# Embedding look-ups in two passes over six small tables, and fourteen loads moved from SyncE's queue to ScalarE's

## The reference

```python
e = jnp.stack([tbl_0[ids[:, 0]], ..., tbl_38[ids[:, 38]]], axis=1)      # (2048, 39, 32)
conv1 = einsum('bid,bjd,ijk->bkd', e, e, W1)                            # 39*39 pairs -> 128
hidden1, final1 = conv1[:, :64], conv1[:, 64:]
conv2 = einsum('bid,bjd,ijk->bkd', e, hidden1, W2)                      # 39*64 pairs -> 128
z = sum(concatenate([final1, conv2], axis=1), axis=2)                   # (2048, 192)
h = relu(concatenate([z, dense_ctx], axis=1) @ W_top1 + b_top1)         # 512
h = relu(h @ W_top2 + b_top2)                                           # 256
y = h @ W_top3                                                          # 1
```

## Time and profile before

| | us |
|---|---|
| median of 3 runs | 811.2 (807.7 to 817.63) |
| the profiled execution | 808.5 |
| span of its core | 806.6 |
| PE busy | 739.2 (92%) |
| VectorE (DVE) busy | 697.9 (87%) |
| ScalarE (ACT) busy | 572.3 (71%) |
| GpSimd (POOL) busy | 543.3 (67%) |

### The profile page before, as it was taken

One profiled execution on the slowest core, in us unless ns is written; L12 is line 12 of the kernel. 1 busy time (PEld: TensorE's weight loads), 2 busy tenths in 40 slices (PEclk: granted clock), 3 DMA queues, 4 the chain that ended last, 5 costly groups with the idle time before them and its releaser, 6 DMA issues.

```text
span 806.6 us, 18279 instructions
## 1 busy us (share of the span) xinstructions
PE 739.2 (92%) x6938; PEld 431.1 (53%) x6938; DVE 697.9 (87%) x1142; ACT 572.3 (71%) x1535; POOL 543.3 (67%) x538
## 2 busy tenths in 40 slices
PE   2991787899999999999999999998999999999997
PEld 1660132375656565655556464655556565656576
DVE  6971986879999999899989898997999999999962
ACT  1330335768888888888887878786888888788883
POOL 6877777777777777777777777777777777700000
PEclk9995986899999999999999999999999999999999
DMA  6738878988898888989898889888898989888500
GB/s 194 233 66 221 241 189 235 254 244 250 253 235 248 239 257 232 262 237 247 228 255 244 243 240 242 241 235 243 232 252 237 252 234 265 248 252 249 158 2 2
DMA packets 135720, 179.32 MB, mean 222 GB/s; under 512 B 105304, under 2 KB 116518, under 8 KB 117648
## 3 DMA queue, kind: packets, MB, share of 16 engines
q1 hardware_dynamic: 111524, 166.84, 71.6%
q0 software_dynamic: 17088, 8.78, 6.6%
q10 hardware_dynamic: 7020, 2.52, 1.2%
HBM read 166.35 MB, written 16.71 MB: 227 GB/s over the span
## 4 chain that ended last, share of the span: by engine, by line
PE 29%; DVE 20%; DMA 20%; ACT 11%; SPq 8%; POOL 6%; issue 6%; ACTq 0%; DVEq 0%; POOLq 0%
DVE blocks L787 18%; DMA copies<-xt 16%; PE hidden L420 14%; SPq L350 7%; PE sums L473 6%; PE sums L447 6%; POOL emb L386 6%; ACT arena L636 5%; DMA xt<-emb 2%; DMA emb<-in_tbl,ids_tile 2%; ACT hid_high L605 2%; PE sums L478 2%; DVE turned L819 2%; ACT xdiag L624 2%; ACT hidden L613 1%
## 5 line engine op out<-in xcount | busy, mean ns | idle before, releaser
L386 POOL DMA_INDIRECT emb<-in_tbl,ids_tile x534 | 543.1, 1017 | 164.8 <-issue 112.5
L787 DVE TENSOR_TENSOR blocks<-copies 117x512 f32<-117x512 f32 x840 | 524.7, 693 | 75.5 <-DMA copies<-xt 59.7
L420 PE MATMUL hidden<-blocks,w_pairs 117*64 117x512 f32 x1792 | 434.6, 614 | 40.3 <-DVE blocks L787 38.4
L636 ACT ACTIVATE arena<-sums 64x480 f32<-64x480 f32 (+2 forms) x936 | 293.0, 313 | 138.6 <-PE sums L447 125.6
L420 PEld LDWEIGHTS hidden<-blocks,w_pairs 117*64 117x64 f32 x1792 | 152.1, 139 | 244.9 <-issue 105.5
L447 PEld LDWEIGHTS sums<-xdiag,turned 64*103 64x103 f32 x2000 | 101.5, 172 | 82.5 <-issue 46.1
L624 ACT ACTIVATE xdiag<-turned 32x468 f32<-32x468 f32 (+1 forms) x256 | 118.8, 464 | 25.7 <-DVE turned L763 22.6
L447 PE MATMUL sums<-xdiag,turned 64*103 64x78 f32 x2000 | 115.4, 262 | 3.3 <-ACT arena L636 2.2
L605 ACT ACTIVATE hid_high<-hidden 32x512 f32<-32x512 f32 x126 | 74.1, 588 | 11.6 <-PE hidden L420 9.7
L473 PE MATMUL sums<-arena,weights 128*64 128x128 f32 x1280 | 78.5, 279 | 0.0
L473 PEld LDWEIGHTS sums<-arena,weights 128*64 128x64 f32 x1280 | 71.1, 139 | 2.4
(11 more groups left out here) (50 smaller groups left out, 258.3 us busy)
## 6 DMA issues: line engine op xcount, KB each, us to landing
copies<-xt SPq DMA_DIRECT2D x448, 312.0 KB
emb<-in_tbl,ids_tile POOLq DMA_INDIRECT x534
xt<-emb SPq DMA_DIRECT2D x32, 152.0 KB
xt<-xt SPq DMA_DIRECT2D x16, 304.0 KB
xt<-emb SPq DMA_DIRECT2D x32, 104.0 KB
blocks<-hot_t SPq DMA_DIRECT2D x6, 512.0 KB, 6.1
xt<-emb SPq DMA_DIRECT2D x32, 56.0 KB
weights<-in_finals SPq DMA_DIRECT2D x1, 1728.0 KB
```

What stands on the lines that cost most here:

```text
L386: pool.indirect_dma_start(out=emb[u][:, f * D:(f + 1) * D], out_offset=None, in_=tables[f], in_offset=bass.IndirectOffsetOnAxis(ap=ids_til ...
L420: mm = nc.tensor.matmul(hidden[64 * c:64 * c + 64, k % 2, bank, :], w_pairs[0:ROWS, t, bank * HALF_HID:bank * HALF_HID + HID], blocks[0:RO ...
L636: op = nc.scalar.activation(out[:, :, cols].rearrange("p h (u b) -> p h u b", u=2), g[rows, i], ACT.Copy)
L787: op = nc.vector.tensor_tensor(blocks[0:ROWS, at + c, :], a[:, cols], b[:, cols], ALU.mult)
```

## The change

- Look-up j is now of table j % 6 and of the half j // 6: six look-ups serve the first 1,024 samples, then six the second. No columns are left out. All six tables are loaded at the start, each with its own place (`copies` 2, 3, 6 and 7), and split once.
- The first tile's hot columns come from the look-ups: ScalarE copies them into `emb[0]` (`hot_first`), and GpSimd gathers 33 tables for tile 0 too, without waits on look-ups.
- Index loads are one for each look-up, half as large, twelve in place of six, with eight buffers.
- There are two keeps, one for each half, in place of three; tile 1's hot rows need the first alone, tile 8's the second.
- The spill of tile 0 stands after all index loads. Within a spill the copy inside `xt` is issued ahead of the wait for the last part's gathers, in every tile.
- ScalarE issues the fourteen copies of chunk 1, after the keep of the second half, all look-ups and tile 0's spill; copy 4, with one buffer, comes last there and waits for step 0 of chunk 0. SP goes from chunk 0's copies to tile 1's hot rows and spill.
- One-hot place 1 is now `copies` 4 and 5; the places go round by three up to the last look-up, which takes place 0.

```diff
-ONES_PLACE = [j % 3 if j < COPIES_FREE else 2 if j % 2 == 0 else 0 for j in range(LOOKUPS)]
+TURNED_FREE = LOOKUPS - 3
+ONES_PLACE = [j % 3 if j < LOOKUPS - 1 else 0 for j in range(LOOKUPS)]
...
-                else:
-                    for m in range(2):
-                        sp.wait_ge(hot_kept[m], 16 * ((KEPT + 1 - m) // 2))
+                if tile in (1, TILES // 2):
+                    sp.wait_ge(hot_kept[tile // (TILES // 2)], 16)
...
-                    sp.wait_ge(gathered[u][s], 16 * gathers(tile, s))
+                    if s < len(PARTS) - 1:
+                        sp.wait_ge(gathered[u][s], 16 * gathers(tile, s))
                     if s == 0 and tile:
                         sp.wait_ge(hot_rows_loaded[u], 16 * hot_loads(tile))
+                    elif s == 0:
+                        sp.wait_ge(hot_first, N_HOT)
                     if s == len(PARTS) - 1:
                         sp.wait_ge(spilled_first[u], 16 * 2 * (p + 1))
...
+                        sp.wait_ge(gathered[u][s], 16 * gathers(tile, s))
...
-                elif chunk == 1:
-                    sp.wait_ge(hot_looked, COPIES_FREE)
-                elif v in (2, 3):
+                elif chunk == 1 or v in (2, 3):
                     sp.wait_ge(hot_looked, LOOKUPS)
...
                 load_hot_rows(1)
-                for v in LOAD_ORDER:
-                    load_copy(0, 0, 1, v)
                 spill(0, 1)
...
-            for f in range(F):
-                if f >= AT_ONCE:
-                    pool.wait_ge(hot_looked, (f - AT_ONCE) // A_LOOKUP + 1)
+            for f in range(N_HOT, F):
                 gather(0, f)
...
             def look_up(j):
-                n = j // 2
+                n = j % N_HOT
...
             def copy_rows(j):
-                n, h = j // 2, j % 2
+                n, h = j % N_HOT, j // N_HOT
                 act.wait_ge(hot_summed, j + 1)
-                if n >= 4 and n % 2 == 0 and h == 0:
-                    act.wait_ge(hot_kept[n // 2 % 2], 16 * (n // 4))
+                if h == 0:
+                    nc.scalar.activation(emb[0][:, n * D:(n + 1) * D], sums[:, j % 4, 0:D], ACT.Copy).then_inc(hot_first, 1)
...
+            def load_second_chunk():
+                act.wait_ge(spilled[0], 16 * SPILLS)
+                act.wait_ge(hot_looked, LOOKUPS)
+                for v in sorted(LOAD_ORDER, key=lambda v: len(x_copy[v]) == 1):
+                    if len(x_copy[v]) == 1:
+                        act.wait_ge(multiplied, pairs_done(0, COPY_USES[v][-1], BANKS - 1))
+                    for g, r in enumerate(ROTATION[v]):
+                        act.dma_start(x_copy[v][1 % len(x_copy[v])][g::THIRDS, :],
+                                      xt[0, r:r + F, 1, :]).then_inc(copied[v][1 % len(x_copy[v])], 16)
```

More of the change, by code:

```diff
@@ L138, in build @@
         y_col = sb("y_col", [P, TILES], F32)
-        rows = sb("rows", [P, 2, TILES, 2, D], F32)
+        rows = sb("rows", [P, 2, TILES // 2, N_HOT, D], F32)
         row_number = sb("row_number", [P, 18], F32)
@@ L176, in build @@
         hot_consts_loaded = sem("hot_consts_loaded")
-        hot_raw_loaded = [sem(f"hot_raw_loaded{n}") for n in range(2)]
+        hot_raw_loaded = [sem(f"hot_raw_loaded{n}") for n in range(N_HOT)]
         hot_unpacked = sem("hot_unpacked")
@@ L185, in build @@
         hot_copied = sem("hot_copied")
+        hot_first = sem("hot_first")
         hot_kept = [sem(f"hot_kept{m}") for m in range(2)]
@@ L258, in gathers @@
             part = PARTS[s]
-            each = part.stop - max(part.start, N_HOT)
-            return each * (tile // 2 + 1) if tile % 2 else part.stop - part.start + each * (tile // 2)
+            return (part.stop - max(part.start, N_HOT)) * (tile // 2 + 1)
         def hot_loads(tile):
@@ L278, in _, with index @@
             sp.wait_ge(hot_stored, 16)
[L280 to L283, removed]
+            def index(j):
+                if j >= INDICES:
+                    sp.wait_ge(ones_ready, ONES_BEFORE[j - INDICES + 1])
+                h = j // N_HOT
+                sp.dma_start(hot_index[j], hot_t[j % N_HOT, h * HALF_B:(h + 1) * HALF_B].partition_broadcast(P)
+                             ).then_inc(hot_index_loaded[j % INDICES], 16)
             def load_hot_rows(tile):
@@ L353, in first_tile @@
             def first_tile():
-                for n in range(N_HOT):
-                    index(n)
-                    if n == 1:
+                for j in range(LOOKUPS):
+                    index(j)
+                    if j == 3:
                         sp.dma_start(ids_tile[1][:, :], ids_t[1]).then_inc(ids_loaded[1], 16)
-                    if n == 4:
+                    if j == INDICES:
                         sp.dma_start(weights[:, 0:N_FIN], finals).then_inc(fin_loaded, 16)
-                    if n == 5:
+                    if j == INDICES + 1:
                         sp.dma_start(weights[:, N_FIN:], layers).then_inc(mlp_loaded, 16)
-                    spill(0, 0, [s for s in range(len(PARTS)) if FIRST_SPILLED[s] == n])
+                spill(0, 0)
                 sp.wait_ge(spilled[0], 16 * SPILLS)
@@ L391, in _ @@
             pool.wait_ge(ids_loaded[0], 16)
-            for f in range(F):
-                if f >= AT_ONCE:
-                    pool.wait_ge(hot_looked, (f - AT_ONCE) // A_LOOKUP + 1)
+            for f in range(N_HOT, F):
                 gather(0, f)
             pool.wait_ge(ids_loaded[1], 16)
-            for at, f in enumerate(range(N_HOT, F)):
-                pool.wait_ge(hot_looked, (F - AT_ONCE + at) // A_LOOKUP + 1)
+            for f in range(N_HOT, F):
                 gather(1, f)
@@ L533, in look_up @@
                     for bank in range(BANKS):
-                        skip = P if j % 2 == 0 and bank == 0 else 0
-                        mm = nc.tensor.matmul(hidden[0:3 * D, j % 2, bank, skip:512], upper[n][:, c, :],
-                                              hot_ones[j][:, c, bank * 512 + skip:(bank + 1) * 512],
+                        mm = nc.tensor.matmul(hidden[0:3 * D, j % 2, bank, :], upper[n][:, c, :],
+                                              hot_ones[j][:, c, bank * 512:(bank + 1) * 512],
                                               start=(c == 0), stop=(c == HOT_C[n] - 1))
@@ L543, in add_parts @@
                     pe.wait_ge(hot_copied, j - 3)
-                for t in range(0 if j % 2 else 1, TILES // 2):
+                for t in range(TILES // 2):
                     mm = nc.tensor.matmul(sums[:, j % 4, t * D:(t + 1) * D], staged[j % 2][:, t * P:(t + 1) * P],
@@ L760, in turn_x @@
                     dve.wait_ge(hot_rows_loaded[u], 16 * hot_loads(tile))
+                else:
+                    dve.wait_ge(hot_first, N_HOT)
                 if since(tile, 2):
@@ L874, in _ @@
                 indices_to_ones(j)
-                if j % 2 and j // 2 + 2 < N_HOT:
-                    split(j // 2 + 2)
+                if j + 2 < N_HOT:
+                    split(j + 2)
             def add_swapped():
```

86 lines of the change are left out of this document (36 added, 50 removed).

## The result

The median of 20 runs is 820.9 us (811.61 to 830.56) against 811.99 us for the kernel before in the same series (20 runs, 807.7 to 818.8). The ratio is 1.0095, with an interval from 1.007 to 1.0119: slower by 1%, where 802 us and a range of 793 to 814 were forecast. That is less than the 2% that the chances went by, but the sign is sure. Single executions of either kernel were sometimes disturbed; they are left out of every ratio, and the profile shown here is one of the changed kernel taken again, undisturbed (span 820.5 us, time 822.28 us).

The account below looks back on a forecast made before the run. PE and DMA nearly both bound the steady part; the start is a chain of gathers, spill and loads. 808.5 - 8.6 - 0 to 1 = 799.5 us profiled, about 802 us as median (2.7 us higher); range 793 to 814.

Parts of the forecast that it names:

- Six gathers less: Start, GpSimd: tile 0 needs 33 gathers instead of 39, the last issued at 49.72 instead of 58.12, 8.4 us earlier.
- The step on the look-ups: Start, VectorE and PE: hot columns in the first tile's buffer at 47.5 us, twelfth look-up ended at 64.9 us.
- so nothing waits there: Tile 1's hot-row load on SP: it needs only the first keep, so no wait was expected.
- The fourteen loads on ScalarE: Chunk 1's copies: issuing them on idle ScalarE is free and saves 10.8 us of SP's queue; tile 1's spill passes them.
- The rule on arbitration: DMA engines go round-robin over rings with work, so the second queue stretches chunk 0: 806 us by it, 802 without.
- rival 1: Even sharing of the two queues during chunk 0: its step 4 waits to 90 us, 806 us total; chance 0.20.
- No long spill issue on SP: Sign that the forecast is right: SP's spill issues are not long; before, two issues of tile 1's spill took 15.53 us.
- C: Cause weighed in the follow-ups, not in the prediction: tile 1's spill is late for a reason of its own; no size.
- The inner copy's 1 us: Every tile's spill: table's inner copy issued ahead of the wait for the last gathers; 1 us gained, bounds 0 and 5.
- The sum: Whole kernel: 8.6 us from the second tile plus 0 to 1 us, about 802 us, 1.1% below; chance 0.55.
- Rival 3: Tile 1's gathers starved by three busy queues: chunk 2's copies 9.7 us late, 821 us total; chance 0.08.
- Rival 2: More than the shift: chunk 2 starts at 110 us and PE keeps its clock through chunk 3, 793 us; chance 0.13.

Follow-up runs that it names:

- the paced kernel: Changed kernel, with VectorE's one-hot set j waiting from the fourth set on for PE's look-up j - 2: 800.66 us (0.9854), in a longer series 805.66 us (0.9908).

## Why the prediction was wrong

**The step that failed is "Six gathers less".** It took the 33rd gather's time, 49.72 us, from the rows of the kernel before, as if GpSimd's pace belonged to GpSimd. It belonged to VectorE's pauses as well, and the change took those away through ONES_PLACE, a line that the prediction did not price at all. The step on the look-ups counted the sets on VectorE and PE and asked nobody else. One gather took 19.49 us, so that the 33rd was issued at 66.26, and that is the 15 us between 57.4 and 72.50. With the pause back the step comes out: copies at 58.99.

The Trainium skill's page "SBUF — State Buffer", section "SBUF: two separate sides", has a mechanism for the stalled gather: VectorE and GpSimd share one pair of ports under an exclusive lock, and while VectorE runs in a mode that takes both ports, GpSimd can't write the descriptors of its DMAs. The trace agrees in direction, and the rate of the sets speaks for a fast mode (1,024 elements per partition in 0.41 us, where a multiply in f32 takes 0.63 us for 512). The 32 multiplies in f32, at the slower rate, that hold up no gather speak for it as well. It differs in extent: by the page the lock is held for the whole instruction, and here the gather was held over some fifty back-to-back instructions until a pause, while others got through such a run. The sets in another form, with nothing else changed, were not tried, so that the lock is the cause is not shown; that VectorE's run of sets without pauses is, the runs with the pause and with the third place show from both sides. Why one gather is caught and its neighbour is not stays open.

**A second step failed: "so nothing waits there"**, on tile 1's hot rows. It asked only for the keep ahead of the load and not for the queue that the load stands in. SP waited 29.7 us for these rows in the changed kernel and 11.7 with the pause back, where it was 0.4 before. With chunk 1's copies on SP the wait is gone, and chunk 2's copies go out 5.1 us earlier (119.41), though chunk 0's go out 1.1 us later (73.64).

**The look-ups were right**: part 0 of the spill at 48.62 (the hot columns at 47.5 were forecast), the end of the twelfth look-up on PE at 65.76 (64.9 was forecast).

**The fourteen loads on ScalarE** were free to issue, as said. The rule on arbitration that the prediction weighed (the Trainium skill, "DMA: Bandwidth & Descriptors", "Queues, rings and completion order") agrees with the trace where both queues start together, at 72.50: 17.9 us in place of 9.7 until the first multiply. It doesn't where SP's queue has a lead, as rival 1 assumed: in the paced kernel SP's copies start at 58.99 and ScalarE's at 68.34, the first multiply comes 10.6 us after the first copy, and from 78.97 on chunk 0 runs through without a wait, so that its step 4 began near 84 and not at 90. What the lead changes is not shown. The price in time of sharing, which rival 1 put at 4 us, can't be told from nothing. "No long spill issue on SP" was a wrong mark, and the reading behind it, that SP's queue was full of copies, does not hold: with the pause, chunk 0's fourteen copies had all landed when step 4 began near 84, and the four issues of tile 1's spill still last from 82.85 to 102.92. So the spill did not pass chunk 1's copies, which was the point of moving them, and chunk 2's copies come at 108.87 where 105.5 was forecast. What holds these issues up stays open. C is thus a limit that the kernel before has too (48.65 us from chunk 0's first copy to chunk 2's, 49.88 with the pause); the changed kernel without the pause makes it worse (52.0).

**The inner copy's 1 us** is below what can be measured, as its bounds of 0 and 5 allowed.

**The sum** was not far off once the pause is back, 800.66 and 805.66 us for 802, but that is partly luck. Chunk 2's first multiply, forecast at 115.7 with VectorE ready and 7 us of stalls to spare, comes at 123.78, because VectorE idles 11.47 us ahead of chunk 1; that is 0.5 us before the 124.32 of the kernel before. The gain arises behind it: VectorE turns the third tile's x at 164.34 in place of 171.68. Ahead of that turning, from 118 us on, it waits 2.2 us for copies and 1.0 for PE, where the kernel before waited 10.1 and 3.6. Chunk 2's copies, 5.3 us earlier than before, are there when VectorE comes to chunk 2. What was missing is a term of about 13 to 20 us: the ratios 1.0065 and 1.0095 of the changed kernel and 0.9854 and 0.9908 with the pause are 1.6 to 2.4% apart. Rival 3 had the right sign and a time of 821 us, but for another reason, so that its time fits by chance: it starved tile 1's gathers by a third queue, and the runs show a gather of tile 0 held up by VectorE, with the fourteen loads on SP as well (20.29 us for one gather). Rival 2 shows in part: in the paced kernel the clock from 160 to 180 us is 1.00 where it was 0.87 before; how much of the 1 to 1.5% comes from there was not separated.

The kernels with the one-line pause are the fastest, 0.9 to 1.5% faster than the kernel before, and can't be told from one another; the change as made is 1% slower.

## What to carry to other kernels

The rate of an engine in the trace of before is a fact of that schedule. Before a step moves by "fewer instructions at the old rate", look at what the other engines did in that stretch, and whether the change makes one of them run on without pauses: here one place more removed a wait that had been doing good. When one GpSimd instruction grows from 1 to 19 us with no semaphore behind it, lay the neighbours' timelines beside it and see whose pause it ends at. And a total that comes out near its forecast does not show that the path was the forecast one: look up where in the trace the gain arises, here between the second and the third tile and not at the second's start.

## What was not expected of the hardware

GpSimd's gathers (indirect DMA issues, mostly of 0.94 to 1.3 us) took up to 20.29 us while VectorE ran one-hot sets without pauses, and ended 0.12 to 0.21 us after VectorE paused or turned to another form of instruction; in the kernel before, with splits and waits between the sets, the longest was 2.07 us. In the longest run of multiplies in f32 without a pause (20.09 us) the gathers took 0.94 to 1.30 us, and in no such run did one take over 2.59 us. Two queues that start together nearly double the time to the first five copies (9.7 to 17.9 us); a queue with a lead of 9 us kept its pace (10.6 us).
